# GpSimd's pieces of late merges three slots back, and a new amount of TensorE filler

## The reference

```python
# block: logmap0 and expmap0 scale each row by a function of its norm
q, k, v = (_to_heads(plin(xm, w, b)) ...)
attn = softmax(einsum('bhqd,bhkd->bhqk', qt, kt) / sqrt(HD))
out_h = expmap0(einsum('bhqk,bhkd->bhqd', attn, vt))
attn_out = plin(_from_heads(out_h), w_o, b_o)      # _from_heads: the "merge"
x = mobius_add(residual, expmap0(g_msa * logmap0(attn_out)))
ff = plin(plin(expmap0(xn * (1 + sc_mlp) + sh_mlp), w_f1, b_f1), w_f2, b_f2)
return mobius_add(residual, expmap0(g_mlp * logmap0(ff)))

# LSTM: 512 steps, each needs the h of the one before
a = xw_t + prev_h @ Wh
i, f, o, g = sigmoid(a[:, :H]), sigmoid(...), sigmoid(...), tanh(...)
next_c = f * prev_c + i * g
next_h = o * tanh(next_c)
```

## Time and profile before

| | |
|---|---|
| median of 3 runs | 1598.03 us (1597.85 to 1598.16) |
| the profiled execution | 1597.94 us, its span 1596.2 us |
| mean granted clock of TensorE | 0.927 of full speed |
| busy, share of the span | PE 91%, PEld 77%, DVE 73%, ACT 57%, POOL 29% |
| steps of the LSTM | the first begins at 304 us of the span, the last at 1590 |
| DMA | mean 12 GB/s |

### The profile page before, as it was taken

How to read it: one execution, slowest core, us unless ns; L and a number is a source line. 1 busy time by engine, 2 the same in 40 slices (tenths; PEclk the granted TensorE clock), 3 DMA queues, 4 the chain that set the end, 5 groups by cost and what they waited for, 6 DMA issues and landing times.

```text
span 1596.2 us, 65234 instructions
## 1 busy us (share of the span) xinstructions
PE 1455.9 (91%) x25337; PEld 1225.1 (77%) x25337; DVE 1161.7 (73%) x6593; ACT 916.1 (57%) x3340; POOL 462.9 (29%) x1230
## 2 busy tenths in 40 slices
PE   3786845899999999999999999999999999999998
PEld 3674533788788888888887878888788888888887
DVE  5998763688878787767777776867676767666665
ACT  2687943767666665656565756565545454544433
POOL 2452121051423333241515151515141413130100
PEclk9996556899999999989999998989999999999999
DMA  8000000000000000000000000000000000000000
GB/s 262 3 1 1 2 1 1 5 3 3 10 3 10 3 9 3 9 3 9 3 10 3 9 3 9 3 3 10 4 9 9 3 9 3 6 3 6 3 6 6
DMA packets 16718, 18.48 MB, mean 12 GB/s; under 512 B 6036, under 2 KB 15384, under 8 KB 16408
## 3 DMA queue, kind: packets, MB, share of 16 engines
q1 hardware_dynamic: 13016, 10.51, 2.2%
q10 hardware_dynamic: 3392, 3.81, 0.8%
HBM read 12.21 MB, written 2.10 MB: 9 GB/s over the span
## 4 chain that ended last, share of the span: by engine, by line
PE 67%; DVE 17%; issue 6%; POOL 5%; ACT 4%; DMA 1%; POOLq 0%; ACTq 0%; DVEq 0%
PE psum L784 23%; PE psum L822 20%; PE psum L759 5%; PE psum L724 4%; PE psum L731 3%; PE psum L659 3%; POOL sc L263 2%; DVE weights L1271 2%; PE psum L671 2%; PE psum L739 2%; PE psum L774 2%; ACT weights L938 1%; DVE gA L1511 1%; DVE gF L1513 1%; POOL sc L429 1%
## 5 line engine op out<-in xcount | busy, mean ns | idle before, releaser
L784 PEld LDWEIGHTS psum<-hl,wh 128*128 128x128 f16 x16384 | 479.9, 96 | 88.6 <-DVE hl L1529 77.3
L784 PE MATMUL psum<-hl,wh 128*128 128x8 f16 x16384 | 515.6, 172 | 7.3 <-DVE hl L1529 5.5
L822 PE MATMUL psum<-zeros,ident 128*128 128x256 f16 x3316 | 452.1, 276 | 7.4 <-DVE gF L1513 2.2
L822 PEld LDWEIGHTS psum<-zeros,ident 128*128 128x128 f16 x3316 | 305.1, 99 | 79.6 <-DVE gF L1513 17.9
L1037 ACT ACTIVATE tA<-gA 128x16 f32<-128x16 f32 x512 | 110.5, 216 | 436.1 <-DVE gA L1511 435.4
L1271 DVE TENSOR_TENSOR weights<-w,weights 128x256 f16<-128x256 f32 x512 | 203.2, 419 | 14.9 <-ACT weights L938 14.7
L1511 DVE TENSOR_REDUCE gA<-psum 128x16 f32<-128x32 f32 x512 | 96.8, 189 | 147.6 <-PE psum L784 141.7
L1527 DVE TENSOR_TENSOR hl<-ot 128x8 f16<-128x8 f32 x512 | 90.1, 176 | 96.1 <-ACT ot L1043 95.5
L944 ACT ACTIVATE w<-psum 128x512 f32<-128x512 f32 x256 | 154.4, 603 | 5.6 <-DVE weights L1271 4.5
L1043 ACT ACTIVATE ot<-cnew 128x8 f32<-128x8 f32 x512 | 109.6, 214 | 82.4 <-DVE cnew L1520 32.5
L938 ACT ACTIVATE weights<-psum 128x512 f16<-128x512 f32 x256 | 153.6, 600 | 3.9 <-PE psum L671 3.9
(11 more groups left out here) (299 smaller groups left out, 2219.6 us busy)
## 6 DMA issues: line engine op xcount, KB each, us to landing
arena<-in_x_dram SPq DMA_DIRECT2D x4, 512.0 KB, 9.0
wf<-in_L_cond_w_f_dram SPq DMA_DIRECT2D x2, 1024.0 KB, 19.3
xr<-in_x_dram SPq DMA_DIRECT2D x64, 32.0 KB, 1.8
out_dram<-place SPq DMA_DIRECT2D x64, 32.0 KB, 1.6
qTs<-in_L_cond_w_ada_dram ACTq DMA_DIRECT2D x1, 1536.0 KB
oT<-in_L_cond_Wh_dram ACTq DMA_DIRECT2D x1, 1024.0 KB, 12.8
wx<-in_L_cond_Wx_dram SPq DMA_DIRECT2D x1, 1024.0 KB, 16.1
rows<-in_L_cond_b_ada_dram ACTq DMA_DIRECT2D x4, 128.0 KB, 14.7
```

The source lines that it names most:

```text
L784: last = mm(cols, wh16[:, half, kc, (g0 + c) * P:(g0 + c + 1) * P], hl[:, :, kc, :, 2].rearrange("p e b -> p b e"), start=False, stop=c == ...
L822: mm(pF[:, D:2 * D], ident16[:], zeros[:], start=False, stop=False, skip_group_check=True)
```

## The change

For the late merges (k >= 8) GpSimd's first part goes from r == 2 to r == 5 and its second from r == 4 to r == 7. VectorE's sum over the heads goes with it from r == 4 to r == 7, and its multiplication by F from r == 8 to r == 10. Other pieces keep their slots. The filler's wanted number becomes 2900 for steps 4 to 63 and 2640 from step 64 on (RAISE stays as it is), and the last filler matmul of a step is only as wide as is still lacking (at least 32 columns), where each had 256.

```diff
-BESIDE, RAISE, HEADS_END = 2750, 4500, 300
+BESIDE, EARLY, RAISE, HEADS_END = 2640, 2900, 4500, 300
...
# GpSimd, merged(k, r), k >= 8
-                if r == 2:
+                if r == 5:
                     hold(pool, "t_rd", 2 * k + 2)
...
-                if r == 4:
+                if r == 7:
                     hold(pool, "m_now", k + 1)
...
# TensorE, keep_busy(t)
-                wanted = RAISE if t < 4 or t % 64 in (0, 1) and t < HEADS_END else BESIDE
-                count = -((beside(t) - wanted) // D)
-                if count > 0:
+                wanted = RAISE if t < 4 or t % 64 in (0, 1) and t < HEADS_END else BESIDE if t >= 2 * RING else EARLY
+                lacking = wanted - beside(t)
+                if lacking > 0:
                     pe.wait_ge(s["l_gF"], t + 1)
-                for i in range(count):
-                    mm(pF[:, D:2 * D], ident16[:], zeros[:], start=False, stop=False, skip_group_check=True)
+                while lacking > 0:
+                    n = min(D, max(lacking, 32))
+                    mm(pF[:, D:D + n], ident16[:], zeros[:, 0:n], start=False, stop=False, skip_group_check=True)
+                    lacking -= n
...
# VectorE, merged(k, r)
-                if r == 4:
+                if r == (4 if k < 2 * B else 7):
                     v.wait_ge(s["m_mn"], k + 1)
...
-                if r == 8:
+                if r == (8 if k < 2 * B else 10):
                     v.wait_ge(s["m_F"], k + 1)
```

## The result

The changed kernel takes 1552.3 us (median of 4 runs, 1551.7 to 1554.69) against 1598.1 us (4 runs), a ratio of 0.971 with a 95% interval of 0.970 to 0.972. The forecast was 1553. The profiled execution takes 1551.88 us, its span is 1550.0.

The account below looks back on a forecast made before the run. A step was bound by the recurrent loop (about 2.31 us) or TensorE's work with filler, plus ScalarE's stall behind clip; 1597.94 - 40.2 - 5.4 + 0.4 = 1552.7, so 1553, range 1548 to 1558 (8 in 10: 1548 to 1565).

Parts of the forecast that it names:

- The moved pieces: Late merges on GpSimd: clip runs ahead of both parts, ScalarE's stall and the half clock go, gaining 40.2 us.
- the window of steps 56 to 63: Undisturbed 8 steps at the same place in their period, 19.6 us at clock 1.00; model for seven of eight stalled windows.
- the eight waits: ScalarE L997 waiting for GpSimd's clip, once per late merge: 3.01 us each, at most 24 us of the gain.
- lower bound: Least gain from moving the merge pieces: only ScalarE's waits go and the clock still falls, 24 us.
- Where a stall could go: Rival, chance 0.06: VectorE waits for F or the sum because GpSimd's part one starts later; 1.5 us a merge gives 1565.
- The filler from step 64 on: TensorE filler cut to 2640 columns with exact tail: saves 5.4 us, bounds 2 and 9, in steps where TensorE is late.
- The 0.076 us a late step: Saving from a narrow tail piece instead of 256 columns, 0.11 less 0.033 us, counted in 119 steps and taken at 60%.
- the 81 ns: Trainium skill's time for a 128-column matmul; as tail cost it would cut the saving to 0.03 us a step; set aside.
- The filler before step 64: TensorE filler at 2900: 76 columns more in at most 60 steps, costing 0.6 less 0.2 us.
- The slower rival: Chance 0.05: the filler's cut lets the clock fall where it held; four cold steps in every period give 1620 us.
- That it feeds itself: Argument for a slower kernel: at half clock TensorE is late in every step, so a clock fall sustains itself.
- The sign of being wrong: VectorE L1347 or L1340 waiting behind GpSimd, or granted clock 0.5 anywhere after step 4.

Follow-up runs that it names:

- one-slot kernel: Kernel before with the new filler and, of the late merges, only GpSimd's second part moved, from r == 4 to r == 5: 1553.8 us, ratio 0.971.
- filler-only run: Kernel before with the new filler widths and counts, merge pieces left at their old slots: 1622.3 us, ratio 1.012.

## Why the prediction was right

**The moved pieces.** Right in mechanism, place and size; the order in GpSimd's queue is shown as the cause by the one-slot kernel, in which nothing else of the merge moves. 40.2 forecast, 39.7 measured alone by the windows, 42 us by the times (1599.9 less 1558.0, on a chip where the kernel before was slower). Each instant of the queue came out within 0.3 us, and the window of steps 56 to 63 was a good stand-in for what the eight would be. One reading was off: I put the eight waits at 24 us from one of them, where the earlier trace rows has 25.8 less 0.3, 25.5. Only the lower bound hung on it.

**Where a stall could go.** I gave VectorE's wait for F a margin of 4 us and a chance of 0.06 to eat it. With r == 10 nothing waits: F is there at 545.1 and VectorE takes it at 548.6, a margin of 3.5 us. But the price that I gave this rival, 1.5 us a merge and 12 us in all, was too low by far: 1.1 us a merge cost 32.

**The filler from step 64 on.** 5.4 us forecast; beside the moved pieces 6.3 measured, from step 64 to the last in the two profiles (1072.0 against 1065.7 us), 5.7 for both filler terms together by the times. The 0.076 us a late step was right: 79 of the 256 steps from 64 to 319 are shorter by more than 0.04 us than with the moved pieces alone, 65 of them by 0.065 to 0.085, where I had reckoned with 60% of 119, and 0.5 us came behind step 320, where I had counted nothing. The filler and the products behind it in one step, before and after (start us, us):

```profile
586.69 0.38 PE L822 MATMUL psum<-zeros,ident 128*128 128x256 f16 x2
586.91 1.00 PE L784 MATMUL psum<-hl,wh 128*128 128x8 f16 x32
```

```profile
582.05 0.31 PE L823 MATMUL psum<-zeros,ident 128*128 128x256 f16 x2
582.20 1.00 PE L784 MATMUL psum<-hl,wh 128*128 128x8 f16 x32
```

From the first filler to the products it was 0.22 us and is 0.15. The argument by which the prediction set the 81 ns aside was weak all the same: the 32 pairs in 1.00 us have 8 columns each and say nothing of pieces of 72 to 80.

But the term was stated as if it stood by itself, and by itself it has the other sign, +22. I priced it at full clock only, where TensorE's columns cost time only if it is late; behind a stall they also decide how long half clock lasts. That is shown by the filler-only run.

**The filler before step 64.** 0.4 us net forecast, 0.2 measured against the kernel before and 0.4 beside the moved pieces. What I did not see is what it is for: with 2640 there, 18 us are lost.

**The slower rival, 0.05.** It did not happen, but the evidence I set against it was weak. I took steps 10 and 11 at 2824 columns in 3.1 us and full clock as proof that 2640 in 2.32 us had 20% to spare. By that count 2500 columns in 2.32 us should hold as well, and they do not. 2640 has less than 140 columns to spare. That two steps had once kept the clock was no proof for 448 of them; the amount had to be tried. So the chance of 0.05 was not earned by its argument, and that the clock held at 2640 was in part luck.

**That it feeds itself** I had as an argument for the rival, and the runs at 2500 and with the filler alone bear it out, up to 58 us at half clock with no stall near, and 62.8 up to the end.

**The sign of being wrong.** I named "0.5 anywhere after step 4". Taken by the letter it is there: the clock falls at 1546.2 us, 2.3 us after the last step's first reduction, as it does in the kernel before at 1594.0. TensorE has nothing left to do by then (PE busy 0.00 in the last 3.7 us), so it costs nothing.

## What to carry to other kernels

When an engine works in order, look at what stands ahead of the instruction that is waited for, not at how long that instruction takes: here a 1.4 us `clip` was late because 3.2 us of work with nobody waiting stood in front of it, and swapping the two gave nearly everything. Price a stall by what the loop loses and with the clock that follows it (1.1 us lost in a step cost 4; a wait of 1.1 us of which the loop lost 0.3 cost no clock), and remove stalls before filler is trimmed: the same cut of 176 columns in most steps gave 5.7 us after and cost 22 before. Where filler holds the clock, find the edge by runs on both sides, and by stretch: the steps before 64 lost the clock at 2640, where those behind kept it.

## What was not expected of the hardware

- A VectorE wait of 1.1 us (once 0.8), nearly all of it lost to the loop, in a loop that else keeps TensorE nearly always busy was followed by 3.4 to 13.7 us at half clock, eight times out of eight. Seven ScalarE waits of 0.3 to 0.4 us, and one of 1.1 us of which the loop lost 0.3, were not.
- Half clock lasted longer with less work per step: behind the same 3 us stall 10.2 us with 2816 to 2824 columns a step and 27.3 us with 2640 (step 184), with TensorE busy almost all of the time in both. It did so behind seven of eight stalls; between 2500 and 2300 it did not.
- From 2640 to 2500 columns a step (with 256 of products beside them) the mean granted clock of the span went from 0.946 to 0.831, and the steps from 64 on took 100 us more.
- The narrow last piece of 80 columns, with its 128x128 weights, takes 35 ns from its start to that of the products behind it where these do not wait, one of 72 columns 32 ns, and a piece of 256 columns 109 ns (the changed kernel's trace). The Trainium skill (TensorE: Matmul & The Clock Gate, section Back-to-back issue gap) gives about 81 ns for a matmul of 128 columns in a stream with weight loads. No filler piece of these two kernels has 128 columns. Taken as an estimate for the narrow piece, it would have made a late step 0.03 us shorter; the traces show 0.07.
